# PSUM banks by a table instead of by kind of step, and five engine orders found anew, in a fused Mamba and attention kernel

## The reference

```python
x = layernorm(x + mamba(x))      # per sequence of 256: u, gate = x@in_w, x@gate_w; causal 4-tap conv; silu;
                                 # delta = softplus((u@dt1_w)@dt2_w); 16 states: h = exp(delta*A)*h + ...;
                                 # y = sum_n C_n h_n + D*u; out = (y*silu(gate)) @ out_w
x = layernorm(x + ffn(x))        # two layers, each:
#   h = shift_token(x); q, k, v = split(h @ wqkv), 8 heads x 64; l2norm, scale, rotary on q, k
#   attention in windows of 64 over the window and the one before; x = x + o @ wo
#   h = layernorm(shift_token(x)); a, g = split(h @ w1 + b1); x = x + (a * gelu(g)) @ w2 + b2
```

## Time and profile before

| | us |
|---|---|
| median of three runs (1068.75, 1068.75, 1062.86) | 1068.75 |
| the profiled execution: span from first to last instruction | 1068.3 |
| PE busy | 929.2 |
| DVE busy | 872.8 |
| ACT busy | 786.6 |
| POOL busy | 695.8 |

### The profile page before, as it was taken

The page is one execution under the profiler, slowest core; times in us unless marked ns, Lnnn a source line. Parts: engine busy times, 40 slices in busy tenths (PEclk is TensorE's granted clock), DMA queues, the critical chain, the costliest instruction groups (busy, mean ns, idle before and its releaser), DMA issues. The chain is left out here.

```text
span 1068.3 us, 25986 instructions
## 1 busy us (share of the span) xinstructions
PE 929.2 (87%) x10152; PEld 560.7 (52%) x10152; DVE 872.8 (82%) x1244; ACT 786.6 (74%) x1897; POOL 695.8 (65%) x386
## 2 busy tenths in 40 slices
PE   5577698899889989999999989998989999987875
PEld 2223345446455565556564646465655666664463
DVE  6788987998889986999999988998898976754542
ACT  5448666886898859886999688877869877783740
POOL 3026615787588775898688859884866677763731
PEclk9788889899999989999999999999999999999986
DMA  7000100010000100000101100100000100110010
GB/s 229 11 6 10 26 1 6 17 33 9 16 16 22 38 20 25 22 24 4 35 12 26 27 13 14 31 21 17 17 22 20 27 6 17 26 27 1 21 31 11
DMA packets 22618, 25.63 MB, mean 24 GB/s; under 512 B 2869, under 2 KB 14815, under 8 KB 22495
## 3 DMA queue, kind: packets, MB, share of 16 engines
q1 hardware_dynamic: 22207, 23.81, 8.6%
q10 hardware_dynamic: 288, 0.14, 0.0%
HBM read 9.26 MB, written 2.10 MB: 11 GB/s over the span
## 5 line engine op out<-in xcount | busy, mean ns | idle before, releaser
L1062 DVE TENSOR_TENSOR_SCAN scan<-du,decay 128x1028 f32<-128x1028 f32 (+1 forms) x160 | 306.3, 1952 | 10.9 <-PE YY L1252 7.3
L768 POOL TENSOR_TENSOR rn<-ssc,expo 128x16 f32<-128x16 f32 x64 | 214.0, 3344 | 5.3
L764 POOL TENSOR_SCALAR ssc<-ss 128x16 f32<-128x16 f32 x64 | 62.4, 975 | 213.4 <-DVE ss L1119 212.8
L914 ACT ACTIVATE prob<-BB,nmax 128x128 f32<-128x128 f32 x472 | 165.7, 380 | 39.4 <-DVE nmax L1157 28.0
L859 ACT ACTIVATE decay<-delta,negA 128x1024 f32<-128x1024 f32 (+1 forms) x160 | 154.2, 986 | 18.4 <-DVE scan L1062 16.5
L773 POOL TENSOR_TENSOR qkc<-qkc,qks 128x1024 f32<-128x1024 f32 x64 | 159.6, 2493 | 2.8 <-DVE qks L1137 2.7
L1252 PE MATMUL YY<-scan,diag 64*64 64x512 f32 (+1 forms) x1280 | 143.1, 538 | 10.9 <-DVE scan L1062 10.9
L777 POOL TENSOR_TENSOR qkc<-qkc,rn 128x1024 f32<-128x1024 f32 x64 | 133.2, 2082 | 5.0
L1252 PE MATMUL AA<-wqkv,hT 128*128 128x512 f32 x256 | 128.8, 627 | 6.0 <-DVE qks L1137 3.1
L914 ACT ACTIVATION_READ_ACCUMULATOR prob<-BB,nmax 128x1 f32 x472 | 104.2, 221 | 0.0
L1119 DVE TENSOR_REDUCE ss<-sq 128x16 f32<-128x1024 f32 x64 | 77.1, 1205 | 29.6 <-ACT sq L877 29.6
(11 more groups left out here) (144 smaller groups left out, 1858.8 us busy)
## 6 DMA issues: line engine op xcount, KB each, us to landing
v_even<-v_odd SPq DMA_DIRECT2D x96, 128.0 KB, 2.3
x<-in_x SPq DMA_DIRECT2D x6, 256.0 KB, 3.4
wqkv<-in_wqkv SPq DMA_DIRECT2D x1, 1536.0 KB
xT<-in_xT SPq DMA_DIRECT2D x6, 256.0 KB, 3.0
out<-outb SPq DMA_DIRECT2D x6, 256.0 KB, 2.9
w<-in_w SPq DMA_DIRECT2D x1, 682.0 KB
xT<-in_xT SPq DMA_DIRECT2D x4, 128.0 KB, 2.6
x<-in_x SPq DMA_DIRECT2D x4, 128.0 KB, 3.5
```

Source lines behind the costliest of these rows:

```text
L768: pool.tensor_tensor(rn[:, q % 2, :], ssc[:, :], expo[:, 0:2 * HEADS], ALU.pow).then_inc(rn_sb, 1)
L914: ins = act.activation(prob[:, h, :], bank_of(q, a)[:, c * P:(c + 1) * P], ACT.Exp, bias=nmax[:, q % 2, h:h + 1], accum_out=den[:, q % 2, ...
L1062: dve.tensor_tensor_scan(state, step, a, 0.0, ALU.add, ALU.mult).then_inc(scan_sb, 1)
```

## The change

HOLDS and LATE go. Two sets of tables name banks per step: PAIR_TABLES, with a letter A, B or Y for each `qk_in`, `qk_T`, `scores`, `probs_T` (64 tiles) and `up_gate` (20 f), and BANK_TABLES, with C or M for `layer_T`, `v_in`, `weighted`, `out_T`, `attn_out`, `shift`, `norm_T`, the third chunk of `up_gate`, each chunk of `up_a`, and `down`. All steps take their tile from `pair`, `bank_of`, `one` or `up_bank` in place of AA, BB, C and M. Y appears from tile 50 and f = 15 on. OWN grows by `shift` after `attn_out`, `norm_T` after `shift`, `down` after its `up_a` chunks. The waits that `free` makes come from a table `release`, with `mamba_sum` of the last group in it as the first holder of YY. The five order tables are new; each has the same steps as before (848, 654, 710, 197 and 89). HELD has 473 entries before and 514 after.

```diff
+PAIR_TABLES = {
+    "qk_in": "ABABABBBAAABAABAABBBAAAAAAABAABBBABABBABAABAAAABABAAABBYAAAYABYB",
+    "qk_T": "AABBABBAAABBABABBBBABAAAAAABABBBABBABABAABBABAAABABBYAYBYAAYBYAY",
+    "scores": "BBAAAABBBABBABAAAAABBBBBBAABAAABAABABABBABBBBABABABAYBYBBBBYAABB",
+    "probs_T": "AABBAABBAAABBBAAABBABABBBAAAAAAABABAAABAAABBBABBBAYAABYYAABYBAAY",
+    "up_gate": "BBABBBBBBBBABBBYAYAB",
+}
+BANK_TABLES = {
+    "layer_T": "CMMMCCMCMCMMCCCMMMMC",
+    "v_in": "MCMCMMCMMMMMMCMMCMCCCMMMCCMCCCCCCCCMCCCMCMCMCCMMCCMMCMCMMMMMCCMM",
+    "weighted": "CCCCCMCCMMCMMCCMMMMCMMMMCCMMCCMCMCMMCMCMCMMCCMCCMMMCMMCMMMCMCMCM",
+    "out_T": "MMCMMMCCMCMMCCCMMMMCMMMCCCMMCCMCMMMCCMCCCMMCCMMCMCMMMCMMMMCMCMCM",
+    "attn_out": "CCMCMCCCMCCCMCMCCMCM",
+    "shift": "MCCCMCCMMCMMCCCCCMMC",
+    "norm_T": "MMCCMMCMMMCCCMCCCCMM",
+    "up_gate": "MCCCMMMMMCMCCCCCMCCC",
+    "up_a": "MMCCCMMMCMCMCCCCMCCMCMCMCMMMMCCMCCMMMCMMCCMCMMMCCCMMCMCMCMCM",
+    "down": "MMMCCCCMMCMMMCMCCCCC",
+}
...
-LATE = [q for q in range(TILE.index((0, GROUPS - 1, 0)), len(TILE)) if q % 2]
-HOLDS = {"qk_in": "A", "qk_T": "B", "scores": "B", "probs_T": "B", "v_in": "C", "weighted": "C", "out_T": "C",
-         "attn_out": "M", "shift": "M", "norm_T": "M", "layer_T": "M", "up_gate": "AM", "up_a": "M", "down": "M"}
-OWN = {"scores": "qk_T", "probs_T": "scores", "out_T": "weighted"}
+def banks_of(step, args):
+    pairs, banks = PAIR_STEPS.get(step), BANK_STEPS.get(step)
+    n = nth(step, args)
+    return (pairs[0][n] if pairs else "") + (banks[0][n] if banks else "")
+OWN = {"scores": lambda q: [("qk_T", (q,))], "probs_T": lambda q: [("scores", (q,))], "out_T": lambda q: [("weighted", (q,))],
+       "shift": lambda f: [("attn_out", (f,))], "norm_T": lambda f: [("shift", (f,))],
+       "down": lambda f: [("up_a", (f, c)) for c in range(NCH)]}
...
+            def release(last, f, *rest):
+                return {
+                    "mamba_sum": lambda: (m_sum, f + 1),
...
             def free(step, *args):
-                for last, (f, *rest) in HELD[step, args]:
...
+                for last, of in HELD[step, args]:
+                    pe.wait_ge(*release(last, *of))
```

More of the change, by code:

```diff
@@ L94 @@
[L94 to L112, removed]
-attn_out 4, probs_T 14, shift 4, v_in 15, state_y 4 4, weighted 13, state_y 4 5, state_y 4 6, norm_T 4, qk_T 15,
@@ new lines @@
+state_y 2 7, state_y 2 8, probs_T 2, shift 0, state_y 2 9, state_y 2 10, scores 3, weighted 2, state_y 2 11, norm_T
+0, up_gate 0, state_y 2 12, state_y 2 13, up_a 0 0, state_y 2 14, probs_T 3, state_y 2 15, up_a 0 1, out_T 2,
+mamba_out 2, weighted 3, u_in 3, out_T 3, up_a 0 2, gate_in 3, layer_T 0 2, v_in 4, qk_in 4, rank 3, qk_in 5,
+step_in 3, down 0, attn_out 1, v_in 5, v_in 6, skip 3, layer_T 1 0, shift 1, v_in 7, qk_T 4, qk_in 6, scores 4,
+state_y 3 0, state_y 3 1, qk_T 5, probs_T 4, norm_T 1, qk_in 7, scores 5, state_y 3 2, weighted 4, state_y 3 3, v_in
@@ new lines @@
+norm_T 2, u_in 4, up_gate 2, up_a 2 0, qk_T 11, gate_in 4, layer_T 0 3, probs_T 10, scores 11, up_a 2 1, out_T 9,
+qk_in 12, rank 4, v_in 12, up_a 2 2, qk_in 13, weighted 10, step_in 4, down 2, probs_T 11, attn_out 3, qk_T 12,
+qk_in 14, layer_T 1 2, skip 4, v_in 13, scores 12, out_T 10, shift 3, state_y 4 0, qk_T 13, weighted 11, state_y 4
+1, qk_in 15, v_in 14, probs_T 12, state_y 4 2, state_y 4 3, scores 13, out_T 11, qk_T 14, weighted 12, qk_in 16,
+norm_T 3, probs_T 13, state_y 4 4, v_in 15, up_gate 3, up_a 3 0, state_y 4 5, scores 14, up_a 3 1, up_a 3 2, qk_T
@@ new lines @@
+v_in 19, out_T 17, qk_T 19, gate_in 5, layer_T 0 4, norm_T 5, scores 19, qk_in 20, v_in 20, rank 5, weighted 18,
+qk_in 21, up_gate 5, step_in 5, up_a 5 0, up_a 5 1, probs_T 19, up_a 5 2, out_T 18, qk_T 20, down 5, qk_in 22, v_in
+21, weighted 19, scores 20, skip 5, qk_T 21, v_in 22, state_y 5 0, out_T 19, qk_in 23, probs_T 20, attn_out 6,
+scores 21, weighted 20, qk_T 22, shift 6, out_T 20, state_y 5 1, state_y 5 2, state_y 5 3, layer_T 1 3, probs_T 21,
+scores 22, v_in 23, qk_in 24, weighted 21, state_y 5 4, norm_T 6, state_y 5 5, state_y 5 6, v_in 24, qk_T 23, v_in
@@ new lines @@
+8, scores 40, state_y 7 9, weighted 39, state_y 7 10, state_y 7 11, state_y 7 12, out_T 39, qk_T 41, v_in 43,
+attn_out 11, probs_T 40, scores 41, shift 11, qk_in 43, weighted 40, state_y 7 13, state_y 7 14, out_T 40, state_y 7
+15, qk_T 42, probs_T 41, norm_T 11, scores 42, mamba_out 7, weighted 41, u_in 8, up_gate 11, out_T 41, probs_T 42,
+gate_in 8, up_a 11 0, up_a 11 1, qk_T 43, layer_T 0 7, up_a 11 2, rank 8, scores 43, step_in 8, qk_in 44, weighted
+42, v_in 44, skip 8, out_T 42, qk_in 45, state_y 8 0, probs_T 43, v_in 45, down 11, weighted 43, state_y 8 1,
@@ L1189, in ffn_norm @@
                 l, g = QUAD[f]
+                rows = tiles(one("shift", f)[:, :])
                 dve.wait_ge(f_rstd, f + 1)
```

590 lines of the change are left out of this document (286 added, 304 removed).

## The result

The kernel after takes 1084.05 us (median of 4 runs, 1079.74 to 1084.74) for 1065.8 of the kernel before on the same chip (4 runs, 1062.86 to 1068.75): a ratio of 1.0156, 95% interval 1.0122 to 1.0189. It is slower by 18 us; the prediction said 1039 us, 30 faster. The profiled execution is the one of 1079.74 us, the fastest of the four; its span is 1077.9. The profiled execution of the kernel before has a span of 1068.3, so the two traces lie 9.6 us apart where the medians lie 18 apart. In every run here whose time and span are both known, the time is 1.7 to 2.0 us above the span; by that the profiled execution of the kernel before took some 1070 us (an estimate), 4 above its median.

What follows compares the result with a forecast made beforehand. TensorE was taken to set the pace from 376 us on, VectorE from 100 to 376. Stage terms 0 - 7 - 15 - 9 and +1 for waits gave -30, so 1068.75 became 1039 us, range 1016 to 1062.

Steps and rivals of the forecast that it cites:

- The arithmetic: Whole kernel: same instructions and sizes on every engine, so no term for changed durations; three more ScalarE table loads taken as 0.
- The theory of slack: Attention tiles on TensorE: shortfalls before dependent steps drop from 69 to 29 us, for bank reuse from 62 to 32.
- 376 to 955 us: -15: Middle stretch, set by TensorE: two thirds of 16.6 us of bank waits go, -11, plus -3 and -1; from +6 to -25.
- 100 to 376 us: -7: Stretch paced by VectorE: a quarter of its 29 us of idle time goes; from 0 to -18.
- To 100 us: 0: Head: step_size 1 some 7 us later, gated 1 5 to 6, made up by scan 2 15; from -6 to +7.
- The tail: -9: From 955 us on: norm_T 17 waits less, -4, and up_a chunks follow sooner, -5; from -3 to -13.
- More waits, +1, and table loads, 0: 41 more TensorE bank waits cost 0 to 5.7 us, taken as 1; three more ScalarE table loads, 3.9 us, taken as covered.
- Rival B: From 376 to 955 us VectorE is the real chain, so only the tail gains: 1064 us; chance 0.17.
- Rival C: Attention and feed-forward steps sharing C and M hold each other up, 163 crossings at 0.27 us, +44: 1083 us; chance 0.07.
- Rival E: Spread pauses lower TensorE's clock in the middle from 0.99 to 0.83: +105, 1144 us; chance 0.03.

Runs made afterwards that it cites:

- dose runs: Both large rotate operations replaced, plus 64 small instructions on one engine: VectorE 1073.27 us (old orders), 1055.81 (new); GpSimd 1055.01 (old), 1047.12 (new).
- both replaced: GpSimd's addition and multiplication in rotate replaced by powers of few columns: 1051.18 us from the kernel before, 1021.2 from the kernel after.

## Why the prediction was wrong

The step that failed is *"The arithmetic stays: same instructions on every engine, same sizes"*: the durations themselves changed with the order, and the sum has no term for it. The theory of slack is borne out by its sign: with the large GpSimd operations replaced the change is worth -30 us. That this is the number forecast is in part luck. By TensorE's count (the 3000th and the 9300th matmul, at 372 and 951 us in the kernel before) the gain lies 1 us in the first part, 7 in the middle and 21 in the tail, where the sum had 7, 15 and 9.

- *The arithmetic.* True of the instructions and wrong of their time. With the same work VectorE got 45 us longer and GpSimd's `rotate` 30. I laid durations of one trace along another order as if they were properties of the instructions; a scan's mean of 2417 ns is made of 2.24 to 2.30 us and of collisions, and an order changes how many. The failed step is worth +48 us (62.9 against 14.6 in the runs: 62.9 - 14.6 = 48), which turns -30 into the +18 measured. The trace of before showed the spread: scans of one shape took from 2.24 to 4.39 us.
- *376 to 955 us: -15, "below lies VectorE's 87%, which allows it".* It did not. VectorE went to 514 of 579 us there, as I read it because a gain of TensorE's packs attention work tighter around the scans; the largest wait became `scan` in front of YY. The dose runs show the second half of the cost: a microsecond of VectorE's busy time costs 0.79 under the new orders and 0.52 under the old, one of GpSimd's 0.46 and 0.10. With both operations replaced this stage goes to 551.7 us of TensorE, against 546.1 under the old orders with both replaced (544.6 in the kernel before), and the gain is 7 us and not 15: the term was too large even then.
- *100 to 376 us: -7.* VectorE's busy time rose by 3.6 us and `gated 4` came at 385 us, not at 365 to 372. With both replaced it came at 370.75, but under the old orders with both replaced at 365.63. VectorE's scans gain nothing here from the new orders, and TensorE gains 1 us by the 3000th matmul: this term was wrong.
- *To 100 us: 0.* `step_size 1` came 9.1 us later (7 predicted), `gated 1` at 84.85 (79 predicted), `gated 2` level as said. But the move of `tables 0` and `masks 0` ahead of `step_size 0`, which stands in the diff, had no price in the text; it is 5.4 us at `step_size 0`, and 2 to 7 at the end.
- *The tail: -9.* Right in its mechanism and too small: behind `gated 9` 206 us became 180 in the kernel after, and behind the 9300th matmul 21 us are won with both replaced, beyond the low end of -13. Behind `gated 9` the clock is 0.97 for 0.94 there and TensorE's busy time 6.3 us less (both replaced); the rest of the 25 us is idle time. The waits of `norm_T 17` for `hn` fell: in the last stretch `hn` in front of L1505 costs 3.4 + 1.9 us for 8.2. And the `up_a` chunks of group 19 (behind the third `up_gate` chunk, the first row) follow each other 0.85 and 0.79 us apart, with no wait for the GELU between, as predicted:

```profile
1066.81 1.06 PE L1279 MATMUL C<-hnT,w 128*85 128x256 f32 x2
1067.66 1.06 PE L1279 MATMUL M<-hnT,w 128*128 128x256 f32 x2
1068.51 0.69 PE L1279 MATMUL C<-hnT,w 128*128 128x256 f32 x2
1069.30 0.66 PE L1279 MATMUL M<-hnT,w 128*85 128x256 f32 x2
```

- *More waits, +1, and table loads, 0*: no row speaks against either; ScalarE's busy time is the same to 0.1 us.
- *Rival B* (VectorE takes it over, 1064) named the right engine but gave VectorE the work of before, and so ended too low by 20. *Rival C* had the number (1083) without being the cause here: the rows in which C or M wait for `hid`, `x` and `hn` add up to 33 us in the kernel after and to 34 before, so they did not grow. Its mechanism is real, as the old orders with 31 moved banks show; I gave it little weight because the orders left 2 us or more at most crossings, and that was sound. *Rival E* did not come: the middle's clock is 0.98, though the banks are cycled more than before.

The chance of 0.08 for slower was too small. It was built from banks and the clock alone, and nothing in it stood for two engines that stop each other. One slip in the working changes nothing: 1.2 us and 8 times 0.60 us are 6.0 us, and less overlap they can't be 6.3.

## What to carry to other kernels

Before durations are laid along a new order, look at their spread within one shape: where the longest is the sum of a scan and of another engine's operation, the duration belongs to the order and not to the instruction. A new order moves the meetings of VectorE and GpSimd, and here it moved the large operations of GpSimd onto the scans; count how often an elementwise GpSimd operation would meet a VectorE operation with both inputs in SBUF, and price each meeting at up to the other operation's whole length, on either engine. And banks from a table and the orders must be found together, with the collision in the cost: under the old orders, 31 moved banks cost 45 us.
